# Queries and keys projected transposed, their stages two quarters later, both subtractions of the split on GpSimd

## The reference, cut to what matters

```python
xn = _layernorm(x)                       # x: (32, 256, 128), float32
qkv = (xn @ Wqkv.T)                      # 16 heads of 8 channels
q = q * cos + _rotate_half(q) * sin      # rotates neighbouring channels
k = k * cos + _rotate_half(k) * sin
scores = einsum('bhqd,bhkd->bhqk', q, k) * scale     # causal, window of 64
y = einsum('bhqk,bhkd->bhqd', softmax(scores), v)
attn = y @ Wproj.T + bproj
# each token's two best of 8 experts: w_e * (gelu(xn @ w1[e] + b1[e]) @ w2[e] + b2[e])
out = x + attn + moe
```

## Time and profile before

| | us |
|---|---|
| median of 3 runs | 761.24 |
| the runs | 761.21, 761.24, 767.58 |
| span of the profiled execution, first to last instruction | 756.8 |
| median less that span | 4.4 |

### The profile page before, as it was taken

One profiled execution on the slowest core, in us unless ns is written; L12 is line 12 of the kernel. 1 busy time (PEld: TensorE's weight loads), 2 busy tenths in 40 slices (PEclk: granted clock), 3 DMA queues, 4 the chain that ended last, 5 costly groups with the idle time before them and its releaser, 6 DMA issues.

```text
span 756.8 us, 26261 instructions
## 1 busy us (share of the span) xinstructions
PE 667.1 (88%) x10171; PEld 523.9 (69%) x10175; DVE 463.1 (61%) x1270; ACT 356.8 (47%) x681; POOL 374.3 (49%) x461
## 2 busy tenths in 40 slices
PE   6778999879888888988889989999999999998984
PEld 3556776656555555655656878989998989986652
DVE  7887877978755755665757644444445444444763
ACT  1446776535444444444446534444344444445561
POOL 2763343446555655555552244545454555444443
PEclk9699999999999999898999999999999999998996
DMA  9589778567776655566558687777767776773987
GB/s 275 175 215 249 222 204 218 157 194 221 198 199 181 172 176 166 153 172 169 155 155 216 195 251 230 225 236 225 256 222 232 224 244 230 234 222 102 311 235 233
DMA packets 156235, 157.92 MB, mean 209 GB/s; under 512 B 20224, under 2 KB 131096, under 8 KB 156112
## 3 DMA queue, kind: packets, MB, share of 16 engines
q1 hardware_dynamic: 141576, 135.29, 62.6%
q0 software_dynamic: 8416, 17.51, 6.8%
q10 hardware_dynamic: 6120, 3.43, 1.7%
HBM read 102.19 MB, written 58.61 MB: 212 GB/s over the span
## 4 chain that ended last, share of the span: by engine, by line
PE 64%; DMA 11%; DVE 10%; issue 10%; SPq 2%; POOL 2%; ACT 0%; another core or an unknown queue 0%; DVEq 0%; ACTq 0%
PE ps L763 12%; PE ps L750 11%; PE ps L698 9%; PE ps L633 5%; PE ps L640 4%; DMA xn<-slots_x 4%; PE ps L606 3%; PE ps L682 3%; DMA chosen_y<-xn,to 3%; PE ps L726 2%; PE ps L675 2%; DVE mx L1003 2%; PE ps L617 2%; PE ps L671 2%; DMA xn<-chosen_y 2%
## 5 line engine op out<-in xcount | busy, mean ns | idle before, releaser
L1003 DVE TENSOR_REDUCE mx<-ps 128x8 f32<-128x1024 f32 x128 | 156.6, 1224 | 115.9 <-PE ps L640 115.4
L1176 ACT ACTIVATE PT<-ps 128x1024 f32<-128x1024 f32 x128 | 131.1, 1024 | 151.6 <-PE ps L682 111.6
L1291 POOL DMA_INDIRECT chosen_y<-xn,to x135 | 129.7, 961 | 140.2 <-DVE xn L1065 113.7
L1198 ACT ACTIVATE hb<-ps,xn 128x256 f32<-128x256 f32 x284 | 112.1, 463 | 148.7 <-PE ps L750 135.6
L1285 POOL DMA_INDIRECT slots_x<-xn,pos x128 | 127.4, 995 | 102.5 <-PE ps L640 80.4
L763 PEld LDWEIGHTS ps<-xn,hb 128*128 128x128 f32 x1080 | 130.8, 192 | 5.3 <-ACT hb L1198 2.3
L763 PE MATMUL ps<-xn,hb 128*128 128x128 f32 x1080 | 132.5, 275 | 0.8 <-ACT hb L1198 0.8
L750 PE MATMUL ps<-xn 128*128 128x256 f32 (+1 forms) x568 | 128.6, 369 | 0.0
L698 PE MATMUL ps<-PT,V 128*32 128x64 f32 (+1 forms) x3072 | 99.5, 250 | 14.4 <-issue 11.8
L750 PEld LDWEIGHTS ps<-xn 128*128 128x128 f32 x568 | 99.1, 190 | 9.9
L698 PEld LDWEIGHTS ps<-PT,V 128*32 128x32 f32 x3072 | 64.1, 114 | 31.1 <-issue 20.3
(11 more groups left out here) (147 smaller groups left out, 868.2 us busy)
## 6 DMA issues: line engine op xcount, KB each, us to landing
xn<-experts SPq DMA_DIRECT2D x71, 578.0 KB
QK<-stack SPq DMA_DIRECT2D x128, 192.0 KB
stack<-sp SPq DMA_DIRECT2D x64, 192.0 KB
xn<-slots_x SPq DMA_DIRECT2D x64, 132.0 KB
stack<-sp SPq DMA_DIRECT2D x64, 128.0 KB
xn<-chosen_y SPq DMA_DIRECT2D x32, 256.0 KB, 5.2
stack<-sp SPq DMA_DIRECT2D x64, 64.0 KB
Vc<-values SPq DMA_DIRECT2D x32, 128.0 KB
```

The source lines that it names most:

```text
L1003: e.tensor_reduce(mo[:, :, :, c, t], ps[:, 0:2, :].rearrange("p g (h k) -> p g h k", k=P), AX.X, ALU.max, negate=True).then_inc(v_mx, 1)
L1176: e.activation(PT[:, u % 2, :], ps[:, stb(u):stb(u) + 2, :].rearrange("p c k -> p (c k)"), ACT.Exp, scale=SCALE).then_inc(a_exp, 1)
L1198: e.activation(hb[:, s, c, 0:m], ps[:, 2 * s + c // 2, (c % 2) * SL:(c % 2) * SL + m], ACT.Gelu, bias=b1b[:, i % NW, c:c + 1]).then_inc(a_ ...
L1291: e.indirect_dma_start(out=Ys, out_offset=bass.IndirectOffsetOnAxis(ap=to[:, i % 4, j:j + 1], axis=0), in_=yb[:, i % 4, j, :], in_offset=N ...
```

## The change

The weights' columns are first put in another order by one copy on GpSimd, so that the projection's stationary operand is a half of the query and key channels and its moving operand 256 tokens: the result comes out with channels on the partitions (queries on 0 to 63, keys on 64 to 127), even channels of each pair in one half of the bank, odd ones in the other. The transposes `turn_qk` are gone, and bank 6 belongs to the layernorm pipeline, to `count` and to the odd expert units. `rest` reads `rc` in SBUF and runs on GpSimd, just ahead of `lo`; `write` issues nine DMAs, each from 64 partitions, in place of six. `FIRST` is -20, `ROUTE` 20; `SOON` is gone. The stages stand at: qk 4b-20, rope 4b-19, add and hi 4b-17, rest, mid and lo 4b-16, write 4b-15, load 4b-13, scores 4b-10.

```diff
-FIRST = -22
+FIRST = -20
-SOON = 12
-ROUTE = 18
+ROUTE = 20
...
-    middle = ((("add", 20), ("out", -4), ("mput", 4), ("residual", -8)), (("hi", 19),),
-              (("norm_y", -6), ("rest", 18), ("mget", 2), ("expand", 2)), (("rope", 21), ("mid", 17)))
-    late = ((("turn_qk", 20), ("lo", 16), ("write", 16)), (("turn_o", -5), ("msplit", 7), ("write", 15)),
...
+    middle = ((("rest", 16), ("out", -4), ("mput", 4), ("residual", -8), ("mid", 16)), (("rope", 19),),
+              (("norm_y", -6), ("mget", 2), ("expand", 2)), (("add", 17), ("hi", 17)))
+    late = ((("qk", 20), ("lo", 16)), (("turn_o", -5), ("msplit", 7), ("write", 15)),
...
-            return (7, 4)[n] if n < 2 else 6 - n % 2
+            return (7, 4)[n] if n < 2 else 6
...
                     for d0, n in ((0, 3), (3, 2), (5, 1)):
-                        e.dma_start(Dv[0, :, d0:d0 + n, :], sp[:, s, 0, 0:n, :]).then_inc(d_w[b % 3], 16)
+                        e.dma_start(Dq[:, 2 * d0:2 * (d0 + n), :],
+                                    sp[0:64, s, 0:n, :].rearrange("p n (o t) -> p (n o) t", o=2)).then_inc(d_w[b % 3], 16)
...
+                        for o in range(2):
+                            e.dma_start(Dk[o, :, d0:d0 + n, :], sp[64:128, s, s0:s0 + 1, o * 256:(o + 1) * 256].broadcast_to(
+                                (64, n, 256))).then_inc(d_w[b % 3], 16)
...
-                    for t in range(2):
-                        c0 = (2 * b + t) * P
-                        k = e.matmul(ps[:, 5, t * 256:(t + 1) * 256], xnT[:, c0:c0 + P], wq_s[:, 0:256], start=True,
-                                     stop=True, skip_group_check=True)
+                    c0 = 2 * b * P
+                    for o in range(2):
+                        k = e.matmul(ps[:, 5, o * 256:(o + 1) * 256], wq_s[:, o, :, :].rearrange("p n h -> p (n h)"),
+                                     xnT[:, c0:c0 + 256], start=True, stop=True, skip_group_check=True)
...
+                elif what == "rest":
+                    b = a[0]
+                    e.wait_ge(v_rc, b + 1)
+                    e.wait_ge(a_hi, b + 1)
+                    if b >= 2:
+                        e.wait_ge(p_lo, b - 1)
+                    e.tensor_tensor(rr[:, b % 2, :], rc[:], sp[:, b % 2, 0, :], ALU.subtract).then_inc(p_rr, 1)
```

More of the change, by code:

```diff
@@ L349, in attention_moe_kernel @@
         d_o, d_one = semaphore("d_o"), semaphore("d_one")
-        e_xt, e_vg, e_rt, e_qk, e_qt, e_sc, e_mt, e_st = (semaphore("e_" + n) for n in (
-            "xt", "values", "route", "qk", "qkT", "scores", "maxT", "scoresT"))
+        e_xt, e_vg, e_rt, e_qk, e_sc, e_mt, e_st = (semaphore("e_" + n) for n in (
+            "xt", "values", "route", "qk", "scores", "maxT", "scoresT"))
         e_pv, e_ot, e_yt, e_pr, e_xs, e_up, e_dn = (semaphore("e_" + n) for n in (
@@ L357, in attention_moe_kernel @@
             "init", "bnstats", "stat", "norm", "xn", "gate", "route", "slots"))
-        v_rb, v_rc, v_rr, v_mx, v_ms, v_rd, v_ys, v_att = (semaphore("v_" + n) for n in (
-            "rope_b", "rope", "rest", "max", "msplit", "recip", "y", "attention"))
+        v_rb, v_rc, v_mx, v_ms, v_rd, v_ys, v_att = (semaphore("v_" + n) for n in (
+            "rope_b", "rope", "max", "msplit", "recip", "y", "attention"))
         v_xs, v_to, v_wt, v_y, v_cmb, v_end, v_pos, v_tb = (semaphore("v_" + n) for n in (
@@ L365, in attention_moe_kernel @@
         a_exp, a_os, a_yt, a_gel = (semaphore("a_" + n) for n in ("exp", "out", "yT", "gelu"))
-        p_init, p_cb, p_nrm, p_xn, p_lo, p_b, p_cmb, p_rt, p_row = (semaphore("p_" + n) for n in (
-            "init", "const", "norm", "xn", "lo", "bias", "combine", "route", "row"))
+        p_init, p_cb, p_wq, p_nrm, p_xn, p_rr, p_lo, p_b, p_cmb, p_rt, p_row = (semaphore("p_" + n) for n in (
+            "init", "const", "queries_keys", "norm", "xn", "rest", "lo", "bias", "combine", "route", "row"))
         block = ctx.enter_context(nc.Block())
@@ L373, in attention_moe_kernel @@
         LOADS_C = 16
+        WRITES = 9 * 16
         LOADS_K = 3 * 16
@@ L592, in _ @@
                     e.wait_ge(p_rt, 6)
-                    for sem, v in b5:
+                    for sem, v in b6:
                         e.wait_ge(sem, v)
-                    e.matmul(ps[:, 5, :], upper if a[0] else onesb, Mb[:], start=True, stop=True,
+                    e.matmul(ps[:, 6, :], upper if a[0] else onesb, Mb[:], start=True, stop=True,
                              skip_group_check=True).then_inc(e_rt, 1)
-                    b5 = [(v_rt, 11 if a[0] else 10)]
+                    b6 = [(v_rt, 11 if a[0] else 10)]
                 elif what == "qk":
@@ L756, in _ @@
                     s = i % 2
-                    bk = 4 + s
+                    bk = 4 + 2 * s
                     e.wait_ge(a_gel, 4 * i + 4)
-                    for sem, v in (b5 if s else b4):
+                    for sem, v in (b6 if s else b4):
                         e.wait_ge(sem, v)
@@ L1308, in _constants @@
     cos, sin = np.cos(fr).astype(np.float32), np.sin(fr).astype(np.float32)
-    d = np.arange(8)
-    sign = np.where(d % 2 == 0, -1.0, 1.0).astype(np.float32)
-    C = np.repeat(cos[:, d // 2], 16, axis=1)
-    S = np.repeat(sin[:, d // 2] * sign, 16, axis=1)
-    C = np.concatenate([C, C], 1).reshape(2, 128, 256).transpose(1, 0, 2).reshape(128, 512)
-    S = np.concatenate([S, S], 1).reshape(2, 128, 256).transpose(1, 0, 2).reshape(128, 512)
+    C = np.tile(np.repeat(cos.T, 16, axis=0), (2, 2))
+    S = np.tile(np.repeat(sin.T, 16, axis=0), (2, 1))
+    S = np.concatenate([-S, S], 1)
     one = np.ones((128, 1), np.float32)
```

76 lines of the change are left out of this document (27 added, 49 removed).

## The result

The changed kernel is slower, by far more than forecast: 840.37 us, median of four runs (835.84 to 843.48), where the kernel before took 764.4 beside it (761.21 to 767.58). The ratio is 1.0985, with a 95% interval of 1.0914 to 1.1056. The forecast was 771.4 with a range to 783. The profiled execution's span is 836.7 us, 79.9 more than before.

The account below looks back on a forecast made before the run. TensorE bounds the full stage, VectorE the routing, a chain of waits the prologue. Terms +1.0 - 1.7 + 7.4 + 1.0 + 2.5 = +10.2 gave a span of 767.0, with 4.4 added 771.4 us; range 750 to 783.

Parts of the forecast that it names:

- The transposes: TensorE drops four transposes a block, but its projection waits 0.72 us for the maxima's copy: +1 us, under the scatters.
- Rest moves: Rest from VectorE to GpSimd: -1.7 us in the routing stage, nothing under the scatters, mid ending under 1 us early.
- The longer way to `load`: Nine DMAs for six at 0.51 us each: 4.5 us of issue in place of 3; reading 64 partitions costs nothing.
- the rival: Full stage: the way to `load` becomes the bound if writes land 2 us later; +8, 779 us, chance 0.11.
- The prologue: Before TensorE is full: first scores at 44.6 delay norm 5 to 48.0 and block 2's scores to 70.0; +7.4 us.
- Two iterations more: Behind the prologue: two more layernorm pipeline iterations fall into the full stage, 0.5 us each; +1.0 us.
- after the experts: Block 31's chain behind the experts: mid stands behind `out`, lo and load come later, scores at 715.3; +2.5 us.

Follow-up runs that it names:

- m2: Changed kernel with writes issued in three parts (behind hi, mid, lo), rest on VectorE and ScalarE's maxima copy ahead of `out`: 730.9 us, ratio 1.032.
- h1: Changed kernel with its nine writes a block issued in three parts, three each behind hi, mid and lo: 750.26 us, ratio 1.065.
- e3: Changed kernel with rest alone moved back from GpSimd to VectorE: 764.7 us, ratio 1.070.
- g7: Kernel before with each of three key writes cut into two of 64 partitions, nine writes a block for six: 736.15 us, ratio 1.039.
- e1: Changed kernel with the stages, FIRST, SOON and ROUTE of the kernel before; new layout and rest on GpSimd stay: 751.26 us, ratio 1.052.
- e2: Changed kernel with the stages of the kernel before and rest on VectorE: 751.36 us, ratio 1.056.
- m1: Kernel before with nine writes a block, all of 128 partitions, in place of six: 725.75 us, ratio 1.025.
- e4: Changed kernel with four idle fp32 transposes ahead of each projection, their result unused: 771.49 us, ratio 1.085.

## Why the prediction was wrong

The direction was right, and so was most of the mechanism in the prologue; the size was an eighth of what came (+10.2 us forecast, +79.9 measured). The direction owes something to luck: it rested on +7.4 us in the prologue, and of the 65.9 us lost behind the prologue the forecast had +2.8. By its own steps:

*The transposes, +1.0.* Right as a reading: the projection waits for the maxima's copy 0.54 us a time (10.7 us, 20 times), forecast 0.72 at the place read. Its worth was small, as said; m2 shows nothing won on the second chips without it, since what stood behind it was the wait for `load`.

*Rest moves, -1.7 and nothing under the scatters.* This step failed. I named the chain (scatters, rest, mid, exponential) and then took "under 1 us to spare" from no row. h1 shows mid waiting 2.9 us and the exponential 1.3 us late, nearly once a block. In the changed kernel as it is, mid waits 29.6 us, 15 times, from block 11's to block 28's scores on the second chip (not at all on the first), and e3 says 2.5 points of the 9.5. VectorE's busy time fell by 7.5 us, not 22: 21.8 went with rest, and small instructions elsewhere took longer.

*The longer way to `load`, priced at 4.5 us of issue, otherwise nothing.* This is the step that failed most. The issue of a write from 64 partitions was taken at the 0.51 us of one from 128; it takes 0.61 to 0.63 by the median, and with the long issues a block's nine last 6.4 us. Worse, the step was counted only where I saw a chain, in the prologue, and left out under the scatters because no row of the kernel before showed a wait there in the blocks I read. g7 puts 29 us into that stage by three writes alone. The rows that would have warned were in reach: in the kernel before `load` was issued 8.4 to 11 us ahead of its scores in the full stage and under the scatters, for most blocks, where it takes about 6 to land. That is 2.5 to 5 us of room, for a way that got 3.2 us of issue longer and had more on GpSimd ahead of it; and SyncE's queue was busy two thirds of the time in the full stage. On the second chips there was less room (6.0 to 8.2 us from block 16 to 28), and there it ran out. I had worked out this very sum for the rival and gave it +8 us and a chance of 0.11.

The Trainium skill ("SBUF — State Buffer", "Door 1: The DMA port swizzle") was weighed there for the landing. No run here shows a landing from 64 partitions that is slow by itself; `load` waited for the writes' landing 3.0 us in the whole profiled execution (2.5 before), on the second chip 8.5 (11.9 before). A rule that I didn't weigh fits what g7 measured: the Trainium skill ("DMA: Bandwidth & Descriptors", "Rules for kernel authors") advises one transfer of 128 partitions in place of two of disjoint halves. Its reason is the shared DMA engines; what g7's trace shows is the issue, 2 x 0.61 us in place of 0.49.

*The prologue, +7.4.* The mechanism was right and the size off. First scores 48.82 (forecast 44.6), norm 5 at 52.48 (48.0), block 2's scores 76.56 with a wait of 3.31 for QK (70.0). The 2.7 us from the last write's beginning to `load` held (39.19 to 41.69 is 2.5). What was mis-sized is the writes themselves: they begin at 32.68 and not at 31.8, and last 7.1 us in place of 4.5, as eight of them take 0.60 to 0.64 us and one takes 1.81. The scores then come 7.1 us behind their load, not 6.1. From norm 5 to lo's end block 2 took the 9.2 us forecast; its nine writes again took 7.0 us (61.72 to 68.67), which is the rest of the difference.

*Two iterations more, +1.0; after the experts, +2.5.* From block 2 to block 10 the changed kernel loses 12.9 us where the forecast had -0.7. On the second chips it is 11.1; the old stages leave 4.8 of it (e1), and three writes alone cost 2.4 (g7). Block 31's scores have a hole of 6.07 us where it was 0.53, from lo's start to `load` it is 11.6 us where it was 8.6, and this part cost 4.8. The experts' stage kept its length, as said.

*What no step had:* the clock. In the profiled execution TensorE is busy 39.5 us longer with less to do, and 29.5 of these lie under the scatters, where it ran at the 1.2 GHz level for 119.5 us and before for 23.9. On the second chip that part is much smaller (7.7 us more busy from block 11 to 28, beside 26.6 more holes). That the clock follows the holes is what the two stretches above suggest; no run here changes the clock alone, so how much of the 79.9 us is clock stays open. Open too is why the kernel before runs 55 us shorter on the second chips, most of it (47) by block 28. And for the first chip itself the cause under the scatters stays open: ahead of a block's first scores TensorE stands still 4.3 us in block 11 and at most 0.8 us in each of blocks 12 to 28, whose loads went out about 10 us before or earlier, so neither the way to `load` nor rest is shown to set the pace there. The total ratio is the same on both; the shares of the parts can differ.

The ratios in one line, each step one part of the change, each against its own chip's runs: nine writes 1.039, the rest of the layout 1.056 (e2), the new stages 1.070 (e3), rest on GpSimd 1.095. The first step and the last stand clear of the noise, and so does the second, narrowly. Between e2 (1.051 to 1.062) and e3 (1.060 to 1.080) the intervals overlap, so what the new stages cost with rest on VectorE isn't told apart from nothing.

## What to carry to other kernels

Count the issuing queue as an engine: so many DMAs by the duration of one issue (the mean, for the median hides the long ones), in each stage, and what of it stands in a row between the last producer and the transfer that the consumer waits for. Issue at each stage what is ready at that stage, rather than all behind the last part; here that alone made the kernel before 1.2% faster and gave back a third of what the change cost. And where a rival's chain has been summed to within a microsecond or two of its limit, it is not a rival with a small chance but may well be the next bound: a saving elsewhere was then worth nothing (m2), and a lengthening showed in the time (g7).

## What was unexpected of the hardware

The time of an issue on SyncE does not follow the bytes: by the median 0.63 us for a query write (192, 128 or 64 KB), 0.61 for a key write of half as much, both from 64 partitions, and 0.49 to 0.50 for the same from 128. On ScalarE the same key write took 0.64. Nor is it fixed for one transfer: the last key write is the same in the kernel before and in m1, and takes 0.51 us there and 0.43 here (medians); why is open. One issue in ten takes over 1 us (27 of 288), and a median doesn't show it. The other surprise is e4: 19 us of useless matmuls on the busiest engine did not make the kernel slower.
